# Team 0's slots sorted by table row, 64 columns of the next MoE round gathered ahead of the last stores, and team 0's early parts added up behind the round's last state

## The reference

```python
for l in range(L):                                    # L = 3, H = 256
    agg = segment_sum(h[src], dst, num_segments=N) / deg
    logits = concatenate([h, agg], -1) @ router_W[l] + router_b[l]
    vals, idx = top_k(logits, 2);  gates = softmax(vals)
    gate_dense = zeros_like(logits).at[rows, idx].set(gates)
    weak = relu(einsum('nh,ehf->nef', agg, weak_W[l]) + weak_b[l])       # 4 experts
    sh = relu(einsum('nh,ehf->nef', agg, strong_W1[l]) + strong_b1[l])   # 4 experts
    strong = einsum('nef,efh->neh', sh, strong_W2[l]) + strong_b2[l]
    moe = einsum('ne,neh->nh', gate_dense, concatenate([weak, strong], 1))
    h = h + sigmoid(h @ conf_W[l] + conf_b[l]) * moe
```

## Time and profile before

| | us |
|---|---|
| median of 3 runs (5831.72 to 5834.1) | 5833.66 |
| span of the profiled execution | 5830.9 |
| PE, DVE, ACT, POOL busy in it | 3215.0, 3413.5, 1201.4, 4155.7 |
| gathers of the MoE rounds: count, mean busy of one | 2400, 0.961 |

### The profile page before, as it was taken

How to read it: one execution, slowest core, us unless ns; L and a number is a source line. 1 busy time by engine, 2 the same in 40 slices (tenths; PEclk the granted TensorE clock), 3 DMA queues, 4 the chain that set the end, 5 groups by cost and what they waited for, 6 DMA issues and landing times.

```text
span 5830.9 us, 59667 instructions
## 1 busy us (share of the span) xinstructions
PE 3215.0 (55%) x11995; PEld 2026.1 (35%) x11995; DVE 3413.5 (59%) x6741; ACT 1201.4 (21%) x2737; POOL 4155.7 (71%) x4323
## 2 busy tenths in 40 slices
PE   4088899999879899989899999200000000000000
PEld 3064555557545555565565566200000000000000
DVE  3255766773657666536566665555565556566563
ACT  1022323333223333323333333200000000000000
POOL 7777777772777777557777766477777767777777
PEclk8579999998889999979999999655555555555555
DMA  4244444441443333233333332222222222222221
GB/s 110 78 138 108 113 113 110 109 109 49 144 108 111 110 109 109 80 114 105 101 104 99 103 96 65 56 59 59 59 59 59 59 46 55 55 56 56 55 56 50
DMA packets 249575, 500.72 MB, mean 86 GB/s; under 512 B 104203, under 2 KB 133444, under 8 KB 249050
## 3 DMA queue, kind: packets, MB, share of 16 engines
q0 software_dynamic: 176592, 446.04, 29.6%
q1 hardware_dynamic: 56234, 33.56, 2.2%
q10 hardware_dynamic: 16608, 19.67, 0.9%
HBM read 464.21 MB, written 34.76 MB: 86 GB/s over the span
## 4 chain that ended last, share of the span: by engine, by line
POOL 25%; PE 22%; issue 16%; DVE 14%; DVEq 13%; DMA 5%; ACT 2%; SPq 1%; ACTq 0%; POOLq 0%
POOL ring L591 22%; PE ps_w1a L1681 4%; PE ps_w1b L1681 4%; PE ps_gate L1706 3%; DMA ring<-gat_tab,stage 3%; PE ps_wide L1706 3%; DVE ps_wide L1139 3%; PE ps_weak_a L1693 2%; PE ps_weak_b L1693 2%; DMA ring<-hidden_tab,stage 2%; DVEq L887 2%; DVE ps_wide L934 2%; DVEq L1171 1%; DVEq L1181 1%; DVEq L1184 1%
## 5 line engine op out<-in xcount | busy, mean ns | idle before, releaser
L591 POOL DMA_INDIRECT ring<-hidden_tab,stage x2400 | 2306.3, 961 | 955.5 <-issue 889.6
L591 POOL DMA_INDIRECT ring<-gat_tab,stage x1600 | 1539.3, 962 | 589.4 <-issue 545.5
L890 DVE TENSOR_TENSOR ps_wide<-ps_wide,ring 128x1024 f32<-128x1024 f32 x450 | 557.8, 1240 | 209.1 <-SPq L418 125.4
L1681 PE MATMUL ps_w1a<-agg_team_t,wbuf 128*128 128x512 f32 (+1 forms) x1248 | 561.6, 572 | 7.3 <-ACT strong L1347 5.9
L1706 PE MATMUL ps_gate<-wbuf,strong 128*128 128x256 f32 x2400 | 559.9, 379 | 0.0
L1810 PE MATMUL ps_w1a<-ident,agg_team_t 128*128 128x128 f32 x28 | 7.8, 434 | 995.0 <-DVE agg_team_t L1217 995.0
L1681 PE MATMUL ps_w1b<-agg_team_t,wbuf 128*128 128x512 f32 (+1 forms) x1248 | 556.0, 568 | 0.0
L1706 PE MATMUL ps_wide<-wbuf,strong 128*128 128x256 f32 x2304 | 537.2, 379 | 0.0
L1706 PEld LDWEIGHTS ps_gate<-wbuf,strong 128*128 128x128 f32 x2400 | 432.6, 190 | 111.2 <-issue 47.7
L1499 ACT ACTIVATE ps_gate<-shifted 128x36 f32<-128x36 f32 x296 | 60.4, 204 | 1859.3 <-DVEq L1128 1846.0
L1706 PEld LDWEIGHTS ps_wide<-wbuf,strong 128*128 128x128 f32 x2304 | 415.3, 190 | 78.5
(11 more groups left out here) (353 smaller groups left out, 4501.6 us busy)
## 6 DMA issues: line engine op xcount, KB each, us to landing
ring<-hidden_tab,stage POOLq DMA_INDIRECT x2400, 2.8
ring<-gat_tab,stage POOLq DMA_INDIRECT x1600, 2.6
hidden_tab<-h_res ACTq DMA_DIRECT2D x24, 512.0 KB, 3.0
hidden_tab<-h_res SPq DMA_DIRECT2D x12, 512.0 KB, 8.1
wbuf<-in_L_gnn_strong_W SPq DMA_DIRECT2D x6, 1024.0 KB, 10.1
wbuf<-in_L_gnn_strong_W SPq DMA_DIRECT2D x12, 512.0 KB, 13.7
gat_tab<-h_res ACTq DMA_DIRECT2D x7, 476.0 KB, 3.7
gat_tab<-h_res ACTq DMA_DIRECT2D x12, 272.0 KB, 2.4
```

The lines of the kernel that those rows point to most:

```text
L591: return pool.indirect_dma_start(out=ring[:, b, 0:width], out_offset=None, in_=table, in_offset=bass.IndirectOffsetOnAxis(ap=stage[:, half ...
L890: nc.vector.tensor_tensor(wide_s, wide_s, rows(u), ALU.add).then_inc(ring_free, 1)
L1681: last = mm(ps_w1[c % 2][:, 0:size * P], w1_w[:, k, s, c * P:(c + 1) * P], agg_team_t[:, k, 0:size * P], start=k == 0, stop=k == 1)
```

## The change

1. **Order of the groups.** The four widest ranked groups become groups 0 to 3, that is team 0; the other 45 are spread with stride 41. The slots of the teams 0 to 12 are then 104, 69, 55, 57, 59, 59, 61, 61, 64, 64, 65, 67 and 13: the same 798 in all, and again 25 rings.
2. **Layout of the tables.** Row g*128+p in place of p*49+g, with one blank row (5632) between the rows of teams 0 to 10 and those of teams 11 and 12. A store of a team now writes 512 runs of 1 KB (544 B in the GAT tables). The second GAT table is stored in 17 pieces in place of 7.
3. **Sorting.** In round 0, between steps 5 and 6, DVE sorts team 0's slots of every node by row number, so that slots whose row lies in the teams 11 and 12 ("late") come last, and counts how many late slots there are at most in each of the four groups. ACT loads the columns for it and stores them into `turn_tab`; PE turns the counts and lays the parts out. Team 0's columns are then four early parts and four late parts. From the inputs the early parts are 26, 17, 15 and 14 columns (72) and the late ones 8 each. If they did not fit, a flag (`apart`) makes both rounds 64 columns longer.
4. **Rounds 1 and 2.** POOL waits for the stores of teams 0 to 10 (`table_early`), gathers two rings (64 columns), then waits for the last two stores (`table_late`). DVE adds up the four early parts right behind the round's last state (`early_part`) into `early_sum`, and the four late parts at the start of the next round (`late_part`). The state of team 10 is stored earlier in step 11, and DVE adds team 10's last expert ahead of the aggregate of group 48.
5. **SP.** In rounds 1 and 2 the weights are loaded after the second ring's gathers in place of the first's.

```diff
+SPREAD, SPREAD_OVER = 41, GROUPS - 4
+LATE_TEAMS = 2
+SOON = (BATCHES - LATE_TEAMS) * TEAM
+BLANK = SOON * P
+CELL = 40
+KEPT = 224
+FIRST_CALL = 2 * RING
+TURN_AT = 6
 # POOL, gathers
+                if 0 < r < LAYERS:
+                    table = whole[0:BLANK + 1, :]
+                    pool.wait_ge(table_early, 16 * (BATCHES - LATE_TEAMS) * r)
+                    rows(0, 0)
+                    rows(0, 1)
+                    table = whole
+                    pool.wait_ge(table_late, 16 * LATE_TEAMS * r)
-                if r < LAYERS - 1:
-                    pool.wait_ge(table_done, 16 * BATCHES * (r + 1))
+                if r == 0:
+                    pool.wait_ge(turned, 1)
+                    apart = pool.value_load(apart_i[0:1, 0:1], min_val=0, max_val=1)
 # SP
-                    load(1, 1)
+                    load(1, 1, head)
                     tell(0)
                     if r:
+                        load(2, 0, head)
+                        tell(1)
                         sp.wait_ge(w2_ready, r * BATCHES * 2 * NS)
 # DVE
+            def early_part(r, j):
+                part_units(r, j)
+                add_slots(early_sum[:, j, :])
+                dve.drain()
+            def late_part(r, j):
+                part_units(r, TEAM + j)
+                nc.vector.tensor_tensor(wide[:, H:2 * H], wide[:, H:2 * H], early_sum[:, j, :], ALU.add)
+                return mean_of(j, r * BATCHES, j)
+            def sort_cells():
+                for i in range(CELL // 8):
+                    for j in range(TEAM):
+                        nc.vector.max(sorted_f[:, j, 8 * i:8 * i + 8], cells[:, j, :])
+                    dve.drain()
+                    if i < CELL // 8 - 1:
+                        for j in range(TEAM):
+                            nc.vector.match_replace(cells[:, j, :], sorted_f[:, j, 8 * i:8 * i + 8], cells[:, j, :], -1.0)
+                        dve.drain()
+                    if after == 1:
+                        add_strong(r, q - 1, NS - 1, TEAM)
                     gather_next(0)
                     if after == 1:
                         fill_up(r)
-                    if tail:
+                    elif tail:
                         add_strong(r, q - 1, NS - 1, TEAM)
                 for j in range(TEAM):
-                    done = aggregate(r, 0, j)
+                    done = late_part(r, j) if r else aggregate(r, 0, j)
-                with dve.Fori(1, TEAMS - 1) as q:
+                with dve.Fori(1, TEAMS - 1 if r else TURN_AT) as q:
                     step(q, TEAM, TEAM)
+                if r == 0:
+                    dve.drain()
+                    count_late()
+                    sort_cells()
+                    apart = place_parts()
+                    with dve.Fori(TURN_AT, TEAMS - 1) as q:
+                        step(q, TEAM, TEAM)
                 add_strong(r, TEAMS, NS - 1, 1)
+                if r < LAYERS - 1:
+                    for j in range(TEAM):
+                        early_part(r + 1, j)
 # ACT
-                act.dma_start(hidden_tab[r + 1][0:NP, :].rearrange("(p g) n -> p g n", p=P)[:, bass.ds(q * TEAM, size), :],
-                              h_res[:, bass.ds(q * TEAM, size), :]).then_inc(table_done, 16)
+                act.dma_start(rows_of_team(hidden_tab[r + 1], q, size), h_res[:, bass.ds(q * TEAM, size), :])\
+                    .then_inc(table_late if late else table_early, 16)
 # PE
+                if r == 0:
+                    pe.wait_ge(late_counted, 1)
+                    nc.tensor.transpose(ps_sum[0:TEAM, 0:P], late4, ident[:]).then_inc(late_turned, 1)
+                    pe.wait_ge(late_known, 1)
+                    mm(ps_tr[:, 0:9], early_w.to_broadcast([TEAM, P]), above[:, 4:13], start=True, stop=False)
```

More of the change, by code:

```diff
@@ L72, with pieces_of @@
 EARLY = (TEAMS - 1) * TEAM
+TURN_AT = 6
+def pieces_of(b):
+    groups = range(b * GBATCH, (b + 1) * GBATCH)
+    return [(q, [g for g in groups if g // TEAM == q]) for q in sorted({g // TEAM for g in groups})]
+PIECES = sum(len(pieces_of(b)) for b in range(GBATCHES))
 LOWEST = -1.5e38
@@ L470, in _ @@
                     continue
-                with sp.Fori(1 if r < LAYERS else 0, bodies // 2) as j:
+                turned_halves = KEPT // RING // 2 if r < LAYERS else 0
+                if r < LAYERS:
+                    with sp.Fori(1, turned_halves) as j:
+                        load(j * 2 + 1, 1, head)
+                        tell(j * 2)
+                        load(j * 2 + 2, 0, head)
+                        tell(j * 2 + 1)
+                with sp.Fori(turned_halves, rounds_of // 2) as j:
                     load(j * 2 + 1, 1)
@@ L605, in attention_rows @@
                     i = bodies * (r - LAYERS) + j * 2 + half
-                    pool.wait_ge(staged[half], loads[half] * (16 * r) + j * 16 + 16)
+                    pool.wait_ge(staged[half], loads[half] * (16 * r) + more + j * 16 + 16)
                     pool.sem_inc(half_begun, 1)
@@ L900, in aggregate @@
                 dve.drain()
-                nc.vector.tensor_reduce(part[:], wide.rearrange("p (s n) -> p n s", n=H), AX.X, ALU.add)
+                add_slots(part[:])
                 dve.drain()
@@ L907, in fill_up @@
             def fill_up(r):
[L909 removed]
+                with dve.Fori(units_before(r) + (apart * LEAD if r else 0) + used, all_of * (r + 1) + (apart * (LEAD * r) if r else 0)) as q:
                     dve.wait_ge(arrived, q + 1)
@@ L1400, in step @@
                         take_agg_t(r, q, size, k)
+                    soon = after < TEAM and r < LAYERS - 1
+                    if soon:
+                        keep_state(r, q - 1, TEAM, late=after == 0)
                     logits_t(r, q, size)
@@ L1409, in step @@
                         take_state(r, q - 1, TEAM)
-                    elif tail:
+                    elif tail and not soon:
                         keep_state(r, q - 1, TEAM)
```

260 lines of the change are left out of this document (207 added, 53 removed).

## The result

The changed kernel takes 5893.11 us (median of 4 runs, 5890.57 to 5894.46); the kernel before, run beside it, 5833.88 (5831.72 to 5841.65). The ratio is 1.0098, 95% interval 1.0086 to 1.011: slower by 59 us, where I had forecast 27. The profiled execution took 5894.46 us and has a span of 5892.9.

What follows compares the result with a forecast made beforehand. PE and POOL were taken as nearly level in the MoE rounds, POOL idling about 90 us behind rounds 0 and 1. Rounds +40, -22, +2, GAT and preparation +4: +24, rounded to +27, 5861 us; range 5826 to 5902.

Steps and rivals of the forecast that it cites:

- A, gathers ahead: Round start to PE's first step: 143.9, 110 and 110 us, with 30 gathers filling 37.5 us of POOL's idle time.
- Sort: Round 0, between steps 5 and 6: counting and sorting on DVE cost 25 us, bounds 10 and 60; PE waits 18.
- B: PE's first step to its step 12 in each MoE round: forecast 955, 948 and 997 us.
- Excess over the recursion: What B takes beyond computed step times: 21, 14 and 8 us in rounds 0, 1 and 2; round 0 bounds 5 and 30.
- the recursion: Each step begins when the step before ends and its columns are gathered: step 12 at 934 us, 989 in round 2.
- S = 77: PE's time in us for a whole team when it waits for nothing, used for rounds 0 and 1; 82 in round 2.
- GAT: GAT rounds: waiting for last stores, in shorter runs, costs 3 us in all, bounds 0 and 10.
- Parts: Eight early and late parts on DVE instead of four groups: costed at nothing, 8 us a round if uncovered.
- Overlap in full: Faster rival: PE's steps without excess and sort hidden, 5786 us, with half of it 5810; chance 0.09 for both.
- dear sort: Slower rival: sorting in round 0 costs 60 us in place of 25, total 5896; chance 0.15.
- nothing seen: Rival of no visible change: sort costs 10 us and small terms nothing, 5839, or 5829 with less excess; chance 0.12.
- The flag: Rival: parts don't fit, so rounds 1 and 2 get 64 columns more, +80 us each, 6021; chance 0.02.

Runs made afterwards that it cites:

- Experiment 2: The changed kernel with POOL waiting for the last two stores before the first gather of rounds 1 and 2, so nothing gathered ahead: 5965.05 us.
- experiment 4: The changed kernel without the copies of row numbers in round 0; later rounds gather only the blank row, so only round 0 is to be read: 7146.86 us.
- experiment 5: The changed kernel without counting and sorting, with constants for the parts' columns: 5865.9 us, ratio 1.0055 to the kernel before.
- experiment 1: The kernel before with only the changed order of the groups, the four widest as team 0: 5919.05 us, ratio 1.0146.
- Experiment 7: The changed kernel with another group order, team 0 of 73 columns, each group wide enough, one ring gathered ahead of the last stores: 5800.36 us, ratio 0.994.
- experiment 6: The changed kernel with team 0 of 65 columns, one ring ahead: 5985.34 us; on a slow chip 8437.95, that order alone in the kernel before 8280.23.

## Why the prediction was right in its direction and wrong in its size

- **A, gathers ahead: right.** 30 gathers, POOL back after 4.7 us, A at 141.0, 111.0 and 110.4 against 143.9, 110 and 110. Experiment 2 prices them at 72 us together (forecast 74 to 75).
- **Sort: right.** 23 us in B of round 0, 27 in the whole (forecast 25; PE waited 22.2 in place of 18). Where DVE's time goes there, in the changed kernel:

```profile
944.66 0.11 DVE L1033 MEMSET x_res<- 128x64 int32 x1
...
951.44 0.51 DVE L1068 MAX8 x_res<-x_res 128x8 f32<-128x40 f32 x4
...
958.03 0.24 DVE L1074 TENSOR_SCALAR x_res<-x_res 128x160 int32<-128x160 f32 x1
...
965.80 0.18 DVE L1112 COPY x_res<-x_res  x1 [1.47 <-issue]
967.44 0.18 DVE L1112 COPY x_res<-x_res  x1 [1.45 <-issue]
```

  Counting takes 6.8 us (forecast 6.5), MAX and MATCH_REPLACE 6.6 (7), the small instructions behind them 2.7 (6) and the copies with their register reads 11 (8). By the Trainium skill's rule of a fixed latency for each instruction (page "VectorE: DVE Perf Modes", section "The TRN2 errata — SBUF-src ops pay a fixed extra latency per instruction") four MAX8 on 40 columns would take 0.41 us with its 58 cycles and 0.79 with its 150, an estimate. The trace has 0.51, nearer the smaller figure. The rule says nothing of the register reads (1.6 us from one L1112 to the next). The 15 us that I made of the sort by the smaller figure leave them out.
- **The step that failed: "Excess over the recursion", "I keep 21 and 14 for rounds 0 and 1".** The excess is what B takes beyond the recursion's 934. I wrote that a PE-bound round is spared some of it, and went by S = 77 in round 0. But there DVE, not PE, sets the step, and without the sort B has an excess of 56 (989.8), where my upper bound was 30. DVE copies the row numbers of each unit; without the copies the step is 76.9 and B 36 us shorter (experiment 4). Even the order alone has B = 975.4, where I had 955. I had noted that "its DVE has the copies of row numbers in every unit", and that DVE has "little room in round 0", but gave this 3 us. It was to be read before. The kernel before, DVE's whole units in round 0, with the copy, and in round 1, without:

```profile
680.76 1.23 DVE L890 TENSOR_TENSOR ps_wide<-ps_wide,ring 128x1024 f32<-128x1024 f32 x1
...
682.60 1.23 DVE L890 TENSOR_TENSOR ps_wide<-ps_wide,ring 128x1024 f32<-128x1024 f32 x1
...
1716.83 1.23 DVE L890 TENSOR_TENSOR ps_wide<-ps_wide,ring 128x1024 f32<-128x1024 f32 x1 [0.34 <-issue]
1718.40 1.23 DVE L890 TENSOR_TENSOR ps_wide<-ps_wide,ring 128x1024 f32<-128x1024 f32 x1 [0.34 <-issue]
```

  A unit takes 1.84 us with the copy and 1.56 to 1.58 without; with 15 units in a team that is 4 us more in a step. Nor were the 21 us of round 0 before "mostly POOL's stalls": POOL waited for others only some 8 us there, 7 of them for DVE, and the rest of its 20 us went into gathers that took longer than 0.94.
- **A second part of it: 14 us in round 0 that are neither order nor sort** (experiment 5). Slower loops around the copies hold some 9.5 of them; why those loops are slower stays open, as do the other 5. In the kernel before such gaps come to 1.3 us in round 0. Together 20 + 14 make the 33 us by which B of round 0 was off, less 2 of the sort.
- **Round 1:** B 954 against 948: the recursion's end is short. PE waits for DVE's aggregate in front of the steps 8 to 11, and DVE for columns (up to 8.5 us in a step). **Round 2:** B 989 against 997: no excess at all where PE is the bound (82.02 us in each step from the third on).
- **GAT: 9 us, not 3, and for another reason.** Both gaps ahead of the GAT rounds are as before (41.8 us from the last state to the first gather against 41.7, and 29.8 against 30.1); the rounds themselves are longer, over half of it by the order (experiment 1). A store of 512 KB in runs of 1 KB lands in 3.3 us in place of 3.0. That agrees with the 0.3 estimated from the Trainium skill's fixed cost of a packet (page "DMA: Bandwidth & Descriptors", section "Why small descriptors are slow (HBM only)"), not with the 5.1 of my other bound.
- **Parts: right, as far as the runs show.** Put at nothing; about 3 us in A, which B gives back (experiment 2).
- **Rivals.** "Overlap in full" fell with round 1's B of 954, over its 940, and with PE's 22 us in front of step 6; "dear sort" and "nothing seen" fell with experiment 5, though the measured time lies next to what the dear sort gave (5896). Whoever had bet on the dear sort would have had the total by luck, with the wrong term. The flag stayed clear.

The sum, corrected, in us of the profiled executions: order +85 in the rounds, GAT +9, rounds 1 and 2 with the gathers ahead against the order alone -70 (1091.3 + 1134.0 against 1126.9 + 1168.3), sort +23, the rest of round 0 +14: 61, against 62 between the two spans. It closes because its terms are differences between the same few traces; what each stands for is shown by the experiments, not by the sum.

## What to carry to other kernels

Compute the steady step for each engine and each round before saying which bounds it: a copy of 0.28 us in a loop of 200 units moves the bound in one round only. And price what a change needs as well as what it brings: only 30 gathers fit ahead, so team 0 needed no more than some 64 columns for them (32 early ones and four late parts of 8), if its groups are wide enough; with 73 the same machinery gives 34 to 42 us, with 104 it loses 59.

## What the runs showed of the hardware

- Gathers that all read one row were slow. In experiment 4, rounds 1 and 2 fetch only the blank row: the median from issue to landing over the whole kernel goes from 2.8 to 12.3 us, the DMA engines' busy share in round 1 from 0.38 to 0.86, and round 1's B from 954 to 1285.

```profile
ring<-hidden_tab,stage POOLq DMA_INDIRECT x2400, 12.3
```

- The same vector loop, instruction for instruction, ran with about 0.6 us or 0.48 us of issue time ahead of its first instruction, and in the changed kernel the longer gap stands in round 0's steps 1 to 5 and not in its steps 6 to 11, which are another copy of the loop in the program. Experiment 7's kernel shows 0.48 in its steps 1 to 5 too. The cause is open.
- A copy with a drain behind it whose offsets are first read from SBUF into registers came every 1.6 us on DVE with two numbers to read (L1112), every 0.97 with one (L1109).
- On two chips the kernel before took 8160 to 8210 us. No trace of it was kept there; the order alone (experiment 6) shows DVE, ACT and POOL busy for as long as elsewhere and idle for the rest. The kernel without a sort was 226 us faster than the kernel before on the first of them and 31 slower on a chip at 5834. A ratio holds for the chip that it was taken on.
